# Splitting the feed-forward weights between the last projections instead of after them, in a fused attention and gated-cell kernel on one core

## The chip, the cores and the metric

One Trainium2 chip, of which the kernel uses one core. The time is device time in microseconds; a comparison is of medians of several runs. The profile is of one execution, taken by the hardware profiler.

## The reference, cut to what matters

Two layers run one after the other over 4096 tokens of width 256. The first is a linear attention with 16 heads of state size 64 whose causal weights are scaled by a decay and by a learned factor for the "level" of each pair (t, s). The second is a gated cell that runs two steps over the two halves of the tokens and then gives an output for each.

```python
Q, K, V, dl = x @ Wq.T, x @ Wk.T, x @ Wv.T, x @ Wdl.T      # per head
W = (Q K^T) * S**-0.5 * decay(t, s) * Lam[level(t, s)]      # causal
x = layernorm(x + layernorm(W V @ Wout.T + x) * g + b)
for xt in (x[0], x[1]):                                    # two steps
    f, i, g = sigmoid(xt@wf.T + c@uf.T + bf), sigmoid(xt@wi.T + c@ui.T + bi), tanh(xt@wc.T + c@uc.T + bc)
    c = f * c + i * g
x = layernorm(x + tanh(x @ wo.T + c @ uo.T + bo))
```

## The kernel before, in words

**Tiles and steps.** The tokens are cut into 32 chunks of 128 (`ci`, NC = 32) and 16 pairs of chunks (`sg`, NSG = 16). All engines run through the same list of steps `s` (STEPS, line 42), four per chunk, NG = 128 steps for the attention, and each engine's program is the order in which it does its part of a step. An engine works strictly in its own order: whatever a waiting instruction stands in front of waits too. PE is TensorE, ACT ScalarE, DVE VectorE, POOL GpSimd, SP the engine that issues every DMA.

**Attention, chunk ci, at step 4ci.** PE `exponents(ci)` (matmuls at L407) needs the transposed level coefficients CT of that chunk, made by DVE's `turn_levels(ci)`, and both halves of the weights W of the chunk before (`d_w`). ACT's `exps(ci)` turns them into E, PE does `weigh(ci-1)` (L439) and `keys(ci)` (transposes, L386), and at step 4ci+1 `scores(ci)` (QT, KT) once ACT has made the first two quarters of E. DVE multiplies scores and E in two halves, `weights(ci, 0)` at step 4ci+1 and `weights(ci, 1)` at 4ci+2. `inter(ci)` (PE L474, then DVE) adds what comes from earlier chunks, with coefficients cB that SP's `load_coefs(sg)` broadcasts from DRAM: one DMA of cT to a scratch (`scr`) and 16 DMAs of cB, issued one after the other, once ACT has written cT at step 8sg-3. `out_proj` (step 4ci+6) and `state(ci)` (PE L503, step 4ci+3) follow.

**Levels of a pair.** GpSimd's `levels(sg, 0)` and `levels(sg, 1)` make AT and prod for the even and the odd chunk of a pair; `token_jobs` puts them at distances 8 and 12 from step 8sg-11, so for the last pair (sg = 15) at steps 117 and 121. DVE's `turn_levels` comes a step later, at 118 and 122, each behind that step's `weights(ci, 1)`.

**Projections.** Q and K of pair sg are made in eight jobs (`project(sg, j)`), each with a product of split weights wH, wL (a high part and a remainder, so that three fast passes stand for one exact product). The last pair's are at steps 111 to 118. `split_x` splits the tokens of a pair out of the buffers xt[0] and xt[1].

**Feed-forward weights.** wH and wL hold the projection weights in the attention and the eight feed-forward matrices (WF, WI, WC, UF, UI, UC, WO, UO, numbers 0 to 7) after it, each in 256 columns. SP loads one matrix at a time into xt[0] or xt[1] (`load_wf`), ACT copies the high part into wH (`split_ffn`), GpSimd subtracts it into wL (`g_wf` counts these). Both do this at steps 119 to 126, matrix n at step 119 + n, at the end of the step. SP loads matrices 0 and 1 in its loop over the pairs, behind `load_coefs(13)` and `load_coefs(14)`, and 2 to 7 after the loop, behind `load_coefs(15)`.

**The seam.** At step 126 PE does `first_bias` (36 products two columns wide, which want six matrices split), at step 127 the first turns of the feed-forward blocks, and from step 128 its gates.

Of the kernel before, what the change touches and what calls it, by code (L numbers as in the profile page):

```python
# [5 lines left out]
P = 128  # L6
F32 = mybir.dt.float32
F32R = mybir.dt.float32r
ALU = mybir.AluOpType
ACT = mybir.ActivationFunctionType  # L10
# [5 lines left out]
NC = NT // P  # L16
# [25 lines left out]
STEPS = range(-3, NG + 13)  # L42
FIRST_FFN = NG - 1


def token_jobs(s):

    out = []
    for d, j in ((12, 7), (0, 0), (0, 1), (1, 2), (3, 8), (5, 3), (7, 4), (8, 5)):
        n = s + 11 - d  # L50
        if n % 8 == 0 and (0 if j == 7 else 1) <= n // 8 < NSG:
            out.append((n // 8, j))
    return out
# [12 lines left out]
def chunk_at(s, d):  # L66

    return (s - d) // 4 if s >= d and (s - d) % 4 == 0 and (s - d) // 4 < NC else None
# [87 lines left out]
def program(nc, x, xT, wqk, wtok, wout, wffn, cst, bcv, fv, out):  # L156
    ctx = ExitStack()
    with ctx:
# [139 lines left out]
        def wcol(n, mt=None):  # L298
            return slice(256 * n + 128 * mt, 256 * n + 128 * mt + 128) if mt is not None else slice(256 * n, 256 * n + 256)
# [4 lines left out]
        @block.sync  # L304
        def _(e):
            def load_x(sg):
                e.dma_start(xs[:, 2 * sg:2 * sg + 2, :], xv[:, 2 * sg:2 * sg + 2, :]).then_inc(l_x[sg], 16)

            def load_xt(sg):
                e.dma_start(xt[sg % 2][:, :, :], kt(xT)[:, :, 256 * sg:256 * sg + 256]).then_inc(l_xt[sg % 2], 16)  # L310

            def load_wf(n):
                e.dma_start(xt[n % 2][:, :, :], wffn.rearrange("(k p) w n -> p k w n", p=P)[:, :, n, :]).then_inc(
                    l_xt[n % 2], 16)

            def load_coefs(sg):

                m, u = MISC["cft", sg, 0]
                e.wait_ge(m_free[m], u + 1)
                e.dma_start(scr.rearrange("a l c t -> (a l) (c t)"), cT[:, :]).then_inc(l_sc, 16)  # L320
                e.wait_ge(l_sc, 16 * sg + 16)
                for c in range(2):
                    ci = 2 * sg + c
                    if ci in INTER:
                        if ci >= 2 and ci - 2 in INTER:
                            for h in range(2):
                                m, u = MISC["inter", ci - 2, h]
                                e.wait_ge(m_free[m], u + 1)
                        for a in range(8):
                            e.dma_start(cB[c][16 * a:16 * a + 16, :, :, :].rearrange("p l u t -> p (l u) t"),  # L330
                                        scr[a, :, c, :].partition_broadcast(16)).then_inc(l_cB[c], 16)

            load_xt(0)
            e.dma_start(wt0, kt(wtok)).then_inc(l_wt, 16)
            e.dma_start(bv[:, 0:B_G], bcv[:, 0:B_G]).then_inc(l_bv, 16)
            for i in (0, 2, 1, 3):
                for k in range(2):
                    c = slice(512 * i, 512 * i + 512)
                    e.dma_start(w0[k][:, c], kt(wqk)[:, k, c]).then_inc(l_wq[i], 16)
                if i == 2:  # L340
                    e.dma_start(cs[:, :], cst[:, 0:C_CT]).then_inc(l_cst, 16)
                    load_xt(1)
            e.dma_start(C[:, :, :].rearrange("p h l -> p (h l)"), cst[:, C_CT:C_END]).then_inc(l_c, 16)
            e.dma_start(wo[:, :, :], kt(wout)).then_inc(l_wo, 16)
            load_x(0)
            e.dma_start(bv[:, B_G:B_END], bcv[:, B_G:B_END]).then_inc(l_b2, 16)
            e.dma_start(fvs[:, :], fv).then_inc(l_b2, 16)
            load_x(1)

            e.wait_ge(p_proj, 8)  # L350
            load_xt(2)
            for sg in range(NSG):
                load_coefs(sg)
                if sg + 3 < NSG:
                    e.wait_ge(g_xl, sg + 1)
                    load_xt(sg + 3)
                if sg + 2 < NSG:
                    load_x(sg + 2)
                if sg >= NSG - 3 and sg < NSG - 1:
                    e.wait_ge(g_xl, sg + 1)  # L360
                    load_wf(sg - NSG + 3)
            for n in range(2, 8):
                e.wait_ge(g_wf, n - 1)
                load_wf(n)
            for n in range(16):
                e.wait_ge(a_out, n + 1)
                if n == 15:
                    e.wait_ge(d_out, 1)
                e.dma_start(ov[:, :, n, :], xs[:, n:n + 17:16, :]).then_inc(l_out, 16)
            e.wait_ge(l_out, 16 * 16)  # L370
# [5 lines left out]
        def wf_landed(n):  # L376
            return 16 * (NSG // 2 + n // 2 + 1)
# [3 lines left out]
        def _(e):  # L381
# [209 lines left out]
            def first_bias():  # L591

                e.wait_ge(a_qk, 8 * NSG)
                e.wait_ge(g_wf, UC + 1)
                e.wait_ge(g_c0, 1)
                for mt in range(2):
                    for n in range(3):
                        c, o = wcol(UF + n, mt), 2 * (3 * mt + n)
                        for k in range(2):
                            t = mm3(banks[0][:, o:o + 2], wH[:, k, c], wL[:, k, c], c0H[:, k, :], c0L[:, k, :],  # L600
                                    k == 0, k == 1)
                t.then_inc(p_b0, 1)
# [146 lines left out]
        def _(e):  # L749
            def act(o, i, f, **kw):  # L750
                return e.activation(o, i, f, **kw)  # L751
# [93 lines left out]
                        e.wait_ge(p_st, STATE[ci - 1] + 1)  # L845
                    act(Kt[:, 512 * n:512 * n + 512], MB[m][:, :], ACT.Copy).then_inc(m_free[m], 1)

            def split_ffn(n):
                e.wait_ge(l_xt[n % 2], wf_landed(n))
                if n == 0:  # L850
                    e.wait_ge(p_proj, 8 * NSG)
                act(wH[:, :, wcol(n)], xt[n % 2][:, :, :], ACT.Copy).then_inc(a_wf, 1)

            def turn_block(blk, t):
                i = blk % 2
# [83 lines left out]
            for s in STEPS:  # L939
                if 0 <= s < NG and s % 4 == 0:  # L940
                    exps(s // 4)
                if (sg := split_x_at(s)) is not None:
                    split_x(sg)
                if s == NG - 4:
                    act(c0H[:, :, :], bc(c0, 2, 2), ACT.Copy).then_inc(a_c0, 1)
                if 0 <= s < NG and s % 4 == 0:
                    keys(s // 4)
                for sg, j in project_jobs(s):
                    project(sg, j)
                for sg, j in token_jobs(s):  # L950
                    if j == 5:
                        turn_coefs(sg)
                for sg, j in token_jobs(s):
                    tokens(sg, j)
                if 0 <= s - NG + 9 < 8:
                    split_ffn(s - NG + 9)
                for u in units_at(s):
                    if u[0] == "x" and u[2] == 0:
                        gate(*u[1:])
                    elif u[0] == "c":  # L960
                        gate(u[1], 1, *u[2:])
                    elif u[0] == "h":
                        gate_h(*u[1:])
                    elif u[0] == "t":
                        turn_block(*u[1:])
                    elif u[0] == "o":
                        if u[1] < 16:
                            outputs(u[1])
                        if 0 <= u[1] - 2 < 16:
                            out_norm(u[1] - 2)  # L970
# [3 lines left out]
        def _(e):  # L974
# [34 lines left out]
            def weights(ci, u):  # L1009
                e.wait_ge(p_sc, 2 * ci + u + 1)  # L1010
                e.wait_ge(a_e, 4 * ci + 4)
                if ci:
                    e.wait_ge(p_y, 2 * ci + u - 1)
                for k in range(2):
                    hs = slice(8 * k + 4 * u, 8 * k + 4 * u + 4)
                    tt(W[:, hs, :], XP[2 * u + k][:, :].rearrange("p (h t) -> p h t", h=4), E[:, hs, :],
                       ALU.mult).then_inc(d_w, 1)
# [286 lines left out]
            for s in STEPS:  # L1304
                if (ci := chunk_at(s, 5)) is not None:
                    turn_y(ci)
                if 0 <= s < NG and s % 4 in (1, 2):
                    weights(s // 4, s % 4 - 1)
                for sg, j in token_jobs(s - 1):
                    if j in (5, 7):  # L1310
                        turn_levels(2 * sg + (j - 5) // 2)
                if (ci := chunk_at(s, 6)) is not None:
                    out_proj(ci)
                if s == FIRST_FFN:
# [32 lines left out]
        def _(e):  # L1347
# [104 lines left out]
            for s in STEPS:  # L1452
# [37 lines left out]
                if (ci := chunk_at(s, 9)) is not None:  # L1490
                    e.wait_ge(d_mv2, ci + 1)
                    root(rs2[:, :], lr2[:, :], mv2[:, 1:2], g_rs2)
                if 0 <= s - NG + 9 < 8:
                    n = s - NG + 9
                    e.wait_ge(a_wf, n + 1)
                    tt(wL[:, :, wcol(n)], xt[n % 2][:, :, :], wH[:, :, wcol(n)], ALU.subtract).then_inc(g_wf, 1)


def constants():
# [70 lines left out]
```

## Time and profile before

| what | value |
| --- | --- |
| median of 3 runs | 691.07 us (690.83 to 691.55) |
| the profiled execution's own time | 691.23 us |
| its span | 689.4 us |
| mean granted clock of PE over the span | 0.981 of full speed |
| PE busy | 667.5 us (97%) |
| DVE, ACT, POOL busy | 473.2 (69%), 339.6 (49%), 348.2 us (51%) |

The profiled execution takes 1.8 us more than its span, for what lies around it. The granted clock is 1.00 at 2.4 GHz and 0.50 at 1.2 GHz. A busy share is an average over stages with different limits, so the stage around the change is read by itself.

### The profile page before, as it was taken

What the parts mean: (1) busy time and instruction counts of PE and PEld (TensorE: products, weight loads), DVE (VectorE), ACT (ScalarE), POOL (GpSimd) and SP (SyncE); (2) the same over time, 40 slices, a digit from 0 to 9 for tenths busy, and PEclk for the clock granted to TensorE, in tenths of its full rate; (3) what the DMA queues carried; (4) which work ended last, traced back from release to release, by engine and by line L of the source; (5) the groups of instructions that cost most, each with busy time, mean ns of one, the idle gap of its engine ahead of it and who ended that gap; (6) DMA issues with size and microseconds to landing.
All of it is one profiled execution on the core that took longest, in us unless ns stands there. A gap on an engine that the chain in (4) does not pass through costs nothing.

```text
span 689.4 us, 22147 instructions
## 1 busy us (share of the span) xinstructions
PE 667.5 (97%) x9194; PEld 604.7 (88%) x9194; DVE 473.2 (69%) x1072; ACT 339.6 (49%) x759; POOL 348.2 (51%) x471
## 2 busy tenths in 40 slices
PE   9799999999999999999999999999978999999994
PEld 7699999999999999899999999999967888888894
DVE  3854877769786868667696868688896435454546
ACT  5545454445545554444455455545433434555555
POOL 2705555646465565656364655655455125343434
PEclk9999999999999999999999999999987899999998
DMA  8112130303131221203031212213032000000002
GB/s 303 40 45 58 41 88 11 98 7 94 30 70 41 60 57 42 68 2 98 8 91 32 68 48 52 69 31 82 3 98 63 1 1 1 31 31 31 31 32 92
DMA packets 53588, 37.09 MB, mean 54 GB/s; under 512 B 5360, under 2 KB 52080, under 8 KB 53488
## 3 DMA queue, kind: packets, MB, share of 16 engines
q1 hardware_dynamic: 53488, 35.67, 19.0%
q8 instruction: 73, 1.20, 0.8%
q14 instruction: 27, 0.22, 0.1%
HBM read 30.41 MB, written 5.24 MB: 52 GB/s over the span
## 4 chain that ended last, share of the span: by engine, by line
PE 90%; DVE 3%; ACT 2%; SPq 1%; DMA 1%; POOL 1%; issue 1%; POOLq 0%; DVEq 0%; ACTq 0%
PE bank L383 66%; PE bank L386 6%; PE bank L407 5%; PE bank L474 5%; PE bank L439 5%; PE bank L503 4%; SPq L330 1%; DMA xt<-in_wffn 1%; DVE t L982 1%; ACT t L751 0%; DVE st L1279 0%; DVE hh L979 0%; DMA scr<-cT 0%; DVE t L979 0%; ACT QT L751 0%
## 5 line engine op out<-in xcount | busy, mean ns | idle before, releaser
L383 PE MATMUL bank<-xH,wH 128*128 128x256 f32 x480 | 144.6, 301 | 0.0
L383 PE MATMUL bank<-xL,wH 128*128 128x256 f32 x480 | 135.0, 281 | 0.0
L383 PE MATMUL bank<-xH,wL 128*128 128x256 f32 x480 | 134.3, 280 | 0.0
L979 DVE TENSOR_TENSOR W<-bank,E 128x512 f32<-128x512 f32 x128 | 82.2, 684 | 34.7 <-PE bank L383 34.7
L383 PEld LDWEIGHTS bank<-xH,wH 128*128 128x128 f32 x480 | 90.5, 189 | 6.3 <-issue 5.5
L383 PEld LDWEIGHTS bank<-xL,wH 128*128 128x128 f32 x480 | 90.7, 189 | 0.4
L383 PEld LDWEIGHTS bank<-xH,wL 128*128 128x128 f32 x480 | 90.5, 188 | 0.0
L751 ACT ACTIVATE E<-bank 128x512 f32<-128x512 f32 x128 | 66.1, 603 | 49.0 <-PE bank L407 49.0
L751 ACT ACTIVATE QT<-bank 128x512 f32<-128x512 f32 x64 | 38.2, 596 | 100.7 <-PE bank L383 100.7
L383 PE MATMUL bank<-QT,KT 64*128 64x128 f32 x1024 | 65.9, 278 | 1.2 <-ACT E L751 1.2
L383 PEld LDWEIGHTS bank<-QT,KT 64*128 64x128 f32 x1024 | 59.7, 188 | 5.6 <-ACT E L751 1.5
L751 ACT ACTIVATE KT<-bank 128x512 f32<-128x512 f32 x64 | 38.0, 594 | 51.7 <-PE bank L383 51.7
L1351 POOL TENSOR_TENSOR lr<-mv,cs 128x1 f32<-128x1 f32 (+1 forms) x80 | 18.3, 228 | 80.8 <-DVE mv L1132 74.9
L1351 POOL TENSOR_TENSOR rs<-lr,cs 128x1 f32<-128x1 f32 (+1 forms) x80 | 51.7, 647 | 6.3
L1351 POOL TENSOR_TENSOR x<-oo,xs 128x256 f32<-128x256 f32 x32 | 23.5, 735 | 60.2 <-DVE oo L982 57.6
L1351 POOL TENSOR_TENSOR t<-t 128x416 f32<-128x416 f32 x42 | 46.6, 1110 | 3.4
L407 PE MATMUL bank<-CT,AT 32*128 32x128 f32 x1024 | 39.1, 291 | 9.3 <-ACT QT L751 5.2
L979 DVE TENSOR_TENSOR g<-g 128x512 f32<-128x512 f32 (+1 forms) x26 | 17.6, 677 | 38.7 <-ACT g L751 38.4
L407 PEld LDWEIGHTS bank<-CT,AT 32*128 32x128 f32 x1024 | 32.9, 193 | 10.6 <-DVE CT L1206 5.3
L1351 POOL TENSOR_TENSOR xL<-xt,xH 128x512 fp32r<-128x512 f32 x15 | 19.1, 1273 | 44.5 <-ACT xH L751 44.5
L751 ACT ACTIVATE t<-t 128x416 f32<-128x416 f32 x64 | 35.3, 552 | 12.6 <-DVE t L1164 7.8
L1351 POOL TENSOR_TENSOR prod<-ll,cs 128x512 f32<-128x512 f32 x32 | 40.7, 1271 | 1.2 <-DVE ll L979 1.2
(151 smaller groups left out, 1686.9 us busy)
## 6 DMA issues: line engine op xcount, KB each, us to landing
cB<-scr SPq DMA_DIRECT2D x240, 64.0 KB, 2.9
xt<-in_xT SPq DMA_DIRECT2D x16, 256.0 KB, 3.0
xs<-in_x SPq DMA_DIRECT2D x16, 256.0 KB, 3.2
out<-xs SPq DMA_DIRECT2D x16, 256.0 KB, 2.1
xt<-in_wffn SPq DMA_DIRECT2D x8, 256.0 KB, 3.1
QT<-in_wqk SPq DMA_DIRECT2D x4, 256.0 KB, 5.8
KT<-in_wqk SPq DMA_DIRECT2D x4, 256.0 KB, 6.1
scr<-cT SPq DMA_DIRECT2D x16, 64.0 KB, 1.9
```

Of the source, the lines that this page charges most:

```text
L330: e.dma_start(cB[c][16 * a:16 * a + 16, :, :, :].rearrange("p l u t -> p (l u) t"), scr[a, :, c, :].partition_broadcast(16)).then_inc(l_cB ...
L383: return e.matmul(o, a, b, start=start, stop=stop)
L386: return e.transpose(o, i, ident)
L407: m = e.matmul(XP[q][:, :].rearrange("p (h t) -> p h t", h=H)[:, :, 8 * j:8 * j + 8], AT[b][r, j, :], CT[b][r, :].rearrange("p (h t) -> p ...
L439: y = e.matmul(YB[32 * n:32 * n + 32, 128 * k:128 * k + 128], V[sg % 3][:, c, v:v + 32], W[:, h, :], start=u == 0 and k == 0, stop=u == 1, ...
L474: t = e.matmul(MB[MISC["inter", ci, k][0]][32 * n:32 * n + 32, 128 * i:128 * i + 128], S[r, l, n, 16 * o:16 * o + 32], QT[b][r, 4 * o + n, ...
L503: t = e.matmul(MB[m][k:k + 64, 16 * q:16 * q + 16], Kt[:, 128 * q + k:128 * q + k + 64], Vw[b][:, c, 128 * h + 16 * q:128 * h + 16 * q + 1 ...
L751: return e.activation(o, i, f, **kw)
L979: return e.tensor_tensor(o, a, b, op)
L982: return e.scalar_tensor_tensor(out=o, in0=a, scalar=s, in1=b, op0=op0, op1=op1)
L1351: return e.tensor_tensor(o, a, b, op)
```

## The change

The eight matrices are split at steps 112 to 119 rather than 119 to 126, in the order [0, 4, 1, 5, 2, 6, 3, 7], so that each goes to the columns which projection job i of the last pair has just read. SP issues loads 2 to 6 of this order ahead of `load_coefs(15)`, and load 7 behind it. For the last pair GpSimd makes the odd chunk's levels at step 119 (distance 10), DVE does both halves of `weights` at step 4ci+1 for the last two chunks, and the last `turn_levels` right behind them at step 121.

```diff
+FIRST_SPLIT = NG - 16
+SPLIT = [0, 4, 1, 5, 2, 6, 3, 7]
 def token_jobs(s):
     for d, j in ((12, 7), (0, 0), (0, 1), (1, 2), (3, 8), (5, 3), (7, 4), (8, 5)):
+        if j == 7 and s > NG - 12:
+            d = 10
         n = s + 11 - d
 # SP
-            def load_wf(n):
-                e.dma_start(xt[n % 2][:, :, :], wffn...[:, :, n, :]).then_inc(l_xt[n % 2], 16)
+            def load_wf(i):
+                if i >= 2:
+                    e.wait_ge(g_wf, i - 1)
+                e.dma_start(xt[i % 2][:, :, :], wffn...[:, :, SPLIT[i], :]).then_inc(l_xt[i % 2], 16)
             for sg in range(NSG):
+                if sg == NSG - 1:
+                    for i in range(2, 7):
+                        load_wf(i)
                 load_coefs(sg)
                 ...
-            for n in range(2, 8):
-                e.wait_ge(g_wf, n - 1)
-                load_wf(n)
+            load_wf(7)
 # PE, first_bias
-                e.wait_ge(g_wf, UC + 1)
+                e.wait_ge(g_wf, 7)
 # ACT
-            def split_ffn(n):
-                e.wait_ge(l_xt[n % 2], wf_landed(n))
-                if n == 0:
-                    e.wait_ge(p_proj, 8 * NSG)
-                act(wH[:, :, wcol(n)], xt[n % 2][:, :, :], ACT.Copy).then_inc(a_wf, 1)
+            def split_ffn(i):
+                e.wait_ge(l_xt[i % 2], wf_landed(i))
+                e.wait_ge(p_proj, 8 * (NSG - 1) + i + 1)
+                act(wH[:, :, wcol(SPLIT[i])], xt[i % 2][:, :, :], ACT.Copy).then_inc(a_wf, 1)
-                if 0 <= s - NG + 9 < 8:
-                    split_ffn(s - NG + 9)
+                if 0 <= s - FIRST_SPLIT < 8:
+                    split_ffn(s - FIRST_SPLIT)
 # DVE
-                if 0 <= s < NG and s % 4 in (1, 2):
+                if 0 <= s < NG - 8 and s % 4 in (1, 2):
                     weights(s // 4, s % 4 - 1)
+                if NG - 8 <= s < NG and s % 4 == 1:
+                    weights(s // 4, 0)
+                    weights(s // 4, 1)
                 for sg, j in token_jobs(s - 1):
-                    if j in (5, 7):
+                    if j == 5 or j == 7 and sg < NSG - 1:
                         turn_levels(2 * sg + (j - 5) // 2)
+                if s == NG - 7:
+                    turn_levels(NC - 1)
 # POOL
-                if 0 <= s - NG + 9 < 8:
-                    n = s - NG + 9
-                    e.wait_ge(a_wf, n + 1)
-                    tt(wL[:, :, wcol(n)], xt[n % 2][:, :, :], wH[:, :, wcol(n)], ALU.subtract).then_inc(g_wf, 1)
+                if 0 <= s - FIRST_SPLIT < 8:
+                    i = s - FIRST_SPLIT
+                    c = wcol(SPLIT[i])
+                    e.wait_ge(a_wf, i + 1)
+                    tt(wL[:, :, c], xt[i % 2][:, :, :], wH[:, :, c], ALU.subtract).then_inc(g_wf, 1)
```

## Rows read from the trace of the kernel before

**Rows 1.** Windows: length, busy us of PE, PEld, DVE, ACT, POOL; PE's clock; DMA.
```profile
440.00:505.00 65.00, 64.70 (x1201) 59.71 (x1200) 52.39 (x127) 30.80 (x71) 36.21 (x51) 1.00 0.20 51
505.00:540.00 35.00, 29.32 (x498) 25.32 (x498) 23.48 (x46) 12.96 (x24) 17.15 (x21) 0.76 0.25 70
540.00:680.00 140.00, 139.89 (x805) 121.52 (x803) 71.20 (x156) 69.35 (x131) 53.26 (x74) 1.00 0.06 21
...
530.00:540.00 10.00, 9.35 (x62) 7.72 (x62) 4.56 (x10) 3.67 (x5) 3.21 (x5) 0.50 0.01 2
```
**Rows 2.** Timeline of PE, steps 120 to 125: start, us, what, [idle before <-releaser].
```profile
502.82 1.17 PE L407 MATMUL bank<-CT,AT 32*128 32x128 f32 x32 [0.30 <-DVE CT L1206]
...
505.96 2.06 PE L383 MATMUL bank<-QT,KT 64*128 64x128 f32 x32
...
510.53 1.11 PE L503 MATMUL bank<-Vw,Kt 128*64 128x16 f32 x32
515.44 2.09 PE L407 MATMUL bank<-CT,AT 32*128 32x128 f32 x32 [3.80 <-DVE CT L1206]
517.46 1.94 PE L439 MATMUL bank<-W,V 128*32 128x128 f32 x32
519.33 1.29 PE L386 MATMUL bank<-cs,KT 128*128 128x128 f32 x8
521.85 2.13 PE L383 MATMUL bank<-QT,KT 64*128 64x128 f32 x32 [1.23 <-ACT E L751]
```
**Rows 3.** Timeline of DVE, steps 115 to 122.
```profile
490.36 0.41 DVE L1136 TENSOR_SCALAR xs<-x,mv,rs 128x256 f32<-128x256 f32 x1
...
504.77 1.44 DVE L1136 TENSOR_SCALAR xs<-x,mv,rs 128x256 f32<-128x256 f32 x1
...
507.38 1.28 DVE L979 TENSOR_TENSOR W<-bank,E 128x512 f32<-128x512 f32 x2
...
512.66 1.29 DVE L979 TENSOR_TENSOR W<-bank,E 128x512 f32<-128x512 f32 x2
...
514.67 0.71 DVE L1206 STREAM_TRANSPOSE CT<-C 128x512 f32<-128x512 f32 x1
```
**Rows 4.** Timeline of ACT, steps 117 to 124.
```profile
499.51 0.36 ACT L751 ACTIVATE cT<-bank 64x256 f32<-64x256 f32 x1
...
514.35 0.63 ACT L751 ACTIVATE wH<-xt 128x512 fp32r<-128x512 f32 x1 [6.74 <-DMA xt<-in_wffn]
...
520.19 0.63 ACT L751 ACTIVATE wH<-xt 128x512 fp32r<-128x512 f32 x1 [4.04 <-DMA xt<-in_wffn]
520.73 2.04 ACT L751 ACTIVATE E<-bank 128x512 f32<-128x512 f32 x4
```
**Rows 5.** Chain of work in order of time: step 116 at full clock, a weight load.
```profile
489.31 1.10 PE bank L407 x32
490.41 1.01 PE bank L439 x32
491.42 1.02 PE bank L386 x8
...
511.40 2.92 DMA xt<-in_wffn
```
**Rows 6.** Timeline of SP's queue: coefficients of the last two pairs, later loads.
```profile
470.14 8.79 SPq L330 DMA_DIRECT2D cB<-scr  x16
...
501.86 9.50 SPq L330 DMA_DIRECT2D cB<-scr  x16
511.40 14.70 SPq L313 DMA_DIRECT2D xt<-in_wffn  x6
```
**Rows 7.** Tile xt from 440 to 540: GpSimd's splits, the loads' landing (min/median/max).
```profile
L1351 POOL TENSOR_TENSOR wL<-xt,wH x8: 1267/1273/1535, 504.8 to 531.2; 128x512 fp32r<-128x512 f32 x8
...
DMA to landing us min/median/max: 2.8/3.1/4.7
```
**Rows 8.** Line L330, every coefficient DMA: ns to issue (min/median/max).
```profile
L330 SPq DMA_DIRECT2D cB<-scr x240: 303/431/1950, 30.6 to 510.9; - x120
```

More of the change, by code:

```diff
@@ L310, in load_xt @@
                 e.dma_start(xt[sg % 2][:, :, :], kt(xT)[:, :, 256 * sg:256 * sg + 256]).then_inc(l_xt[sg % 2], 16)
-            def load_wf(n):
-                e.dma_start(xt[n % 2][:, :, :], wffn.rearrange("(k p) w n -> p k w n", p=P)[:, :, n, :]).then_inc(
-                    l_xt[n % 2], 16)
+            def load_wf(i):
+                if i >= 2:
+                    e.wait_ge(g_wf, i - 1)
+                e.dma_start(xt[i % 2][:, :, :], wffn.rearrange("(k p) w n -> p k w n", p=P)[:, :, SPLIT[i], :]).then_inc(
+                    l_xt[i % 2], 16)
             def load_coefs(sg):
```

## The prediction

> **What bounds the kernel now.** I read windows first, then PE's timeline where it is not full, then who released it, then the queues behind those.
>
> The windows cut the span into attention, seam and feed-forward [rows 1]. PE is busy 64.70 of 65 us before 505 and 139.89 of 140 us after 540, at a granted clock of 1.00; only in the 35 us between them does it stand (29.32 busy) and run slow (0.76). No other engine is full anywhere: DVE has 52.39 of 65 us before 505. So work of ACT and GpSimd costs nothing while it is in time, and what a change can win or lose is in that seam.
>
> PE's timeline of the seam [rows 2] has two holes. The first: the last chunk's exponents stand 3.80 us, until 515.44, for CT. CT is made by the last `turn_levels`, whose transpose starts at 514.67, behind the second W half at 512.66, though the first half was made from 507.38 [rows 3]. The second: `scores(31)` wait 1.23 us, until 521.85, for ACT's E. ACT could have begun E at the end of the exponents but stood in its split of a weight matrix until the load landed: 6.74 us before 514.35, 4.04 us before 520.19, and only then E at 520.73 [rows 4]. The holes cost a third thing: the exponents, `weigh` and `keys` after the first hole take from 515.44 to 520.62 (521.85 less 1.23), 5.18 us, where the same three take 1.10 + 1.01 + 1.02 = 3.13 us at full clock [rows 2, 5]. That is 2.05 us at half the clock (1.2 of 2.4 GHz), right after PE had stood idle.
>
> Together 3.80 + 1.23 + 2.05 = 7.08 us. From `scores(30)` at 505.96 to `scores(31)` at 521.85 are 15.89 us; without the three it is 8.81.
>
> **Part 1: both W halves in step 121, the levels earlier.** The transposed CT of chunk 31 then needs W(30,0), W(30,1), the copy, reduce and transpose, and no longer stands behind `inter(30)` and the second step. From 507.38 that is 2 x 1.28 plus the 1.43 us from the second half's end (512.66 + 1.29) to the transpose's (514.67 + 0.71): ready at about 511.4, when PE's state products end (510.53 + 1.11 = 511.64) [rows 2, 3]. This takes out 3.80 us and the slow clock behind it, 2.05. The d_w wait of the exponents is met at the same moment. Late next is nothing on DVE: DVE's `inter(30)` moves behind 1.3 + 1.4 us of other work, and so does its `state(30)`, which PE's `inter(31)` waits for; but PE has exponents, `weigh`, `keys` and `scores` (3.13 + 2.1 us) in between. Cost zero, with that work as cover, and up to 2.7 us if it is gone.
>
> **Part 2: eight splits moved to steps 112 to 119.** Each issues one ACT copy (0.63 us), one GpSimd subtraction (1.27 us) and one load on SP [rows 4, 7]. ACT gets 5 us and GpSimd 10.2 us more within about 30; they were busy 30.80 and 36.21 of 65 [rows 1]. The gates of loads 2 to 6 are a turn-around of split, load and split, 1.27 + 3.1 + 0.63 = 5.0 us per two steps, and a step is some 3 us (four of them from 502.82 to 515.44 with the hole), so it just keeps up; I let ACT wait up to 1 us in it, which PE's projections hide. With those splits gone from steps 120 to 126, the 1.23 us before `scores(31)` go too.
>
> **Part 3: load 7, and what queues behind it.** This is what decides. SP does its loads in program order: 2 to 6, then `load_coefs(15)`, then 7. `load_coefs(15)` starts when ACT has written cT at 499.51 and ends with 16 issues, 9.50 us from 501.86 to 511.36; the next in the queue, a weight load, is issued at 511.40 [rows 4, 6]. That place, held by matrix 2 before, is now load 7's. It lands 2.92 us later, at 514.33 [rows 5]. But ACT wants it at step 119 and stands there, and behind it in ACT's order are `exps(30)` of step 120, which followed the exponents of 502.82 at once before. Everything of chunk 30 hangs on them:
> - ACT's split at 514.35, next instruction 0.54 later (520.19 to 520.73), so E(30) at 514.89;
> - scores 1.12 after E starts (520.73 to 521.85), so `scores(30)` at 516.01 [rows 2, 4], against 505.96: **+10.05 us**, in which PE has nothing to do (its exponents, `weigh` and `keys` are done by 506);
> - then 8.81 us of work, plus slow clock after a 10 us hole. The hole of 3.80 cost 2.05; I take the same, so `scores(31)` at 526.87 against 521.85: **+5.02 us**.
>
> So the sum is 10.05 - 3.80 - 1.23 - 2.05 + 2.05 = +5.02. From `scores(31)` on both kernels have the same PE work to the first gate; `first_bias` now asks for seven splits, which were done long before. The feed-forward part is full of PE work and only moves. GpSimd's split 7 waits with ACT and holds x1 of chunk 28, whose reader on DVE stands behind W(30) anyway.
>
> **Unknown terms, from both sides.** The 16 issues took 8.79 us for the pair before [rows 6]: -0.7 us. Should ACT's inserted copies make cT late: +0.6 to +1. Landing 2.8 to 4.7 us [rows 7]: -0.1 to +1.8; I take 2.92, the same place in the queue. The slow clock could last longer after a longer hole: at worst as in 530 to 540, where all 10 us ran at 0.50 [rows 1], which is 5 us rather than 2.05, +3; the short stretch is nearer, since dense work follows in both. That slow stretch itself, behind the two-column products of `first_bias`, I keep at its 5 us; were PE back at full clock 4 us after the turns begin, as after the first hole, about 2.5 us come back, and all of it at best.
>
> **Two DVE durations against a rule.** A DVE operation took 0.41 us alone and 1.44 us while GpSimd split a matrix [rows 3]: +1.03. The Trainium skill ("SBUF — State Buffer", section "SBUF: two separate sides") calls the port pair that DVE and GpSimd share an exclusive lock: a GpSimd operation that starts first fully blocks a DVE one with two SBUF inputs. The row agrees in kind; the rule would let each of the eight splits hold DVE for its whole length, 10.2 us, and it speaks against moving them to where PE is full.
>
> **The rivals.**
> - A. *DVE is late before step 117.* Six splits fall there, and at 1.03 us each that is 6.2 us on DVE [rows 3]. DVE's idle share, 12.6 of 65 us, gives back 5.0 of some 26 us [rows 1]. Between 1.2 and 6.2 us would reach PE and shift cT, the coefficients and all that follows; I take 2 us, near the lower end, since PE's dependences on DVE there have steps of slack. Time 691.1 + 5.0 + 2.0 = 698.1. Against: splits after step 117 hide in the new hole.
> - B. *The clock comes back at the seam.* PE is busy longer before `first_bias`, and the slow stretch is shorter or absent: 691.1 + 5.0 - 2.5 = 693.6, or 691.1 with all 5 us back. For: its start is not fixed by a wait. Against: its cause, tiny products, stays.
> - C. *Faster: load 7 is in time.* If it is landed when these exponents end, all of 7.08 us is won: 684.0. The point from which it decides: gain and loss balance when `scores(30)` start 7.08 - 2.05 = 5.03 us late, at 510.99, so with a landing at 509.3. Even with all 16 issues at their fastest, 0.303 + 0.04 us each [rows 8], 5.5 us, load 7 goes out at 507.4 and lands at 510.2. So this needs the queue to be shorter than the code has it, or to combine with B.
> - D. *It does not do what it says*: ACT's wait is covered by something I missed, and the time stays at 691.1.
>
> **How the numbers follow.** The profiled execution (span 689.4, own time 691.23) would become 694.4 and 696.3; it stands 0.16 above the median of 691.07, so the forecast is 691.07 + 5.0 = **696.1 us**. Chances: forecast 0.64, A 0.14, B 0.12 (half of it within 0.2%), C 0.07, D 0.03. A measurement of this kernel tells changes of over 0.2%, 1.4 us. Faster 0.07; same 0.06 + 0.03 = 0.09; slower 0.64 + 0.14 + 0.06 = 0.84. The range takes the forecast with its bounds (-0.8 for the queue, +1.8 for the landing or as much for the clock), A, and the nearer half of B: 693.0 to 699.3; the far half of B, C and D are left out.
>
> **What would show it.** In the profile after: ACT's eighth split starts at about 514.3 with an idle time of 10 to 12 us before it, released by the DMA; PE stands about 10 us before `scores(30)`, put down to ACT's E; no hole before the last L407 group and none before `scores(31)`; a granted clock of 0.50 for some 4 us after 516; the first gate at about 543 instead of 537.9; the feed-forward part as long as before. A hole before 499 would speak for A; an eighth split before 510, or a SP queue that issues it ahead of the cB group, would make the forecast wrong, as would a granted clock of 1.00 right after the hole.

## The result, and the profile after

The changed kernel takes 696.73 us (median of 4 runs, 695.15 to 698.45) against 691.01 us before, a ratio of 1.0082 (95% interval 1.0055 to 1.0109). It is slower by 5.7 us; forecast were 5.0 and 696.1 us. Built and timed a second time it took 697.59 against 691.34 us, 1.0092 (1.0077 to 1.0107).

Of the profiled execution (698.45 us, span 696.7) 2.26 us have nothing to do with the change: the exponents of chunk 29 already start that much later, at 491.50 instead of 489.24 (in the chain of waits 489.31 [rows 5]). Some of it is there at the first exponents of all, where no line differs (35.68 against 34.74 us), behind a load of constants that was awaited until 7.79 us instead of 6.87; and the clock after them was half for longer (mean 0.90 from 40 to 50 us, against 1.00). So I compare **the seam**: from the start of the exponents of chunk 29 to the first gate product. It is 48.70 us before (489.24 to 537.94) and 53.93 after, +5.23.

The windows of after, the seam's end moved with the rest (columns as in [rows 1]):

```profile
440.00:505.00 65.00, 64.79 (x1152) 60.05 (x1150) 53.65 (x124) 34.46 (x79) 42.79 (x55) 1.00 0.25 69
...
505.00:545.00 40.00, 31.49 (x552) 27.92 (x556) 25.56 (x54) 9.78 (x19) 11.53 (x18) 0.73 0.14 35
545.00:685.00 140.00, 140.00 (x804) 121.25 (x797) 69.42 (x151) 68.33 (x128) 51.23 (x70) 0.99 0.06 20
```

Before 505 ACT and GpSimd have 3.7 and 6.6 us more work and PE is as full as it was; after 545 nothing has changed. The loss is in the seam, where PE now stands for 8.5 of 40 us instead of 5.7 of 35. The timeline of PE in it, to be read against [rows 2]:

```profile
491.50 1.17 PE L416 MATMUL bank<-CT,AT 32*128 32x128 f32 x32
...
506.16 2.09 PE L416 MATMUL bank<-CT,AT 32*128 32x128 f32 x32 [1.37 <-DVE CT L1214]
508.18 1.74 PE L448 MATMUL bank<-W,V 128*32 128x128 f32 x32
509.85 1.09 PE L395 MATMUL bank<-cs,KT 128*128 128x128 f32 x8
517.56 3.78 PE L392 MATMUL bank<-QT,KT 64*128 64x128 f32 x32 [6.62 <-ACT E L760]
521.27 2.46 PE L483 MATMUL bank<-QT,S 64*32 64x128 f32 x96
...
524.73 1.11 PE L512 MATMUL bank<-Vw,Kt 128*64 128x16 f32 x32
525.77 1.17 PE L416 MATMUL bank<-CT,AT 32*128 32x128 f32 x32
...
529.19 2.05 PE L392 MATMUL bank<-QT,KT 64*128 64x128 f32 x32
...
545.43 0.80 PE L392 MATMUL bank<-yH,wH 128*128 128x512 f32 x1
```

Both old holes are gone (no wait stands before 525.77 and 529.19). A small one before the exponents of chunk 30 has grown from 0.30 to 1.37 us. A new one of 6.62 us stands before `scores(30)`, released by ACT's E, and the work after it runs slowly: 3.78 us for products that take 2.06. What ACT and SP did meanwhile, from their timelines:

```profile
504.28 0.62 ACT L760 ACTIVATE wH<-xt 128x512 fp32r<-128x512 f32 x1
515.91 0.63 ACT L760 ACTIVATE wH<-xt 128x512 fp32r<-128x512 f32 x1 [11.01 <-DMA xt<-in_wffn]
516.44 2.04 ACT L760 ACTIVATE E<-bank 128x512 f32<-128x512 f32 x4
```
```profile
502.17 0.46 SPq L328 DMA_DIRECT2D scr<-cT  x1
504.13 8.76 SPq L338 DMA_DIRECT2D cB<-scr  x16
512.93 0.43 SPq L321 DMA_DIRECT2D xt<-in_wffn  x1
```

ACT waits 11.01 us for the eighth matrix, whose load SP issues at 512.93, behind the 16 coefficient DMAs. E follows 0.53 us after the split starts, and the scores 1.12 us after E.

### The profile page after: what moved, and what is told of

Read it like the earlier page. It is cut to its first block, busy times and chain, and to the rows that moved or that the text cites. A ratio compares the mean times of both kernels' runs of the same rounds, so it can differ in the third digit from the quotient of the medians.

```text
span 696.7 us, 22154 instructions
## 1 busy us (share of the span) xinstructions
PE 671.2 (96%) x9194; PEld 608.6 (87%) x9194; DVE 474.9 (68%) x1072; ACT 338.9 (49%) x759; POOL 348.5 (50%) x471
## 4 chain that ended last, share of the span: by engine, by line
PE 90%; DVE 3%; ACT 2%; DMA 2%; SPq 1%; issue 1%; POOL 1%; POOLq 0%; DVEq 0%; ACTq 0%
PE bank L392 65%; PE bank L395 6%; PE bank L416 5%; PE bank L483 5%; PE bank L448 5%; PE bank L512 4%; SPq L338 1%; DMA bv<-in_bcv 1%; DVE t L990 1%; ACT t L760 0%; DMA xt<-in_wffn 0%; DVE st L1287 0%; DVE hh L987 0%; DMA scr<-cT 0%; DVE t L987 0%
## 5 line engine op out<-in xcount | busy, mean ns | idle before, releaser
L392 PE MATMUL bank<-QT,KT 64*128 64x128 f32 x1024 | 67.5, 283 | 6.6 <-ACT E L760 6.6
L392 PEld LDWEIGHTS bank<-QT,KT 64*128 64x128 f32 x1024 | 61.3, 192 | 11.0 <-ACT E L760 7.0
L392 PE MATMUL bank<-yH,wH 128*128 128x512 f32 (+1 forms) x102 | 40.2, 394 | 0.0
```

Source lines behind the costliest of these rows:

```text
L392: return e.matmul(o, a, b, start=start, stop=stop)
```

## The experiments

The theory: ACT's order puts E of chunk 30 behind a split that waits for a load which is last in SP's queue. Its rivals: DVE and GpSimd, loaded by the moved splits, are the bound; or the part that should win is worth something else than its hole. The table gives each run's seam beside its time, and how much of the seam lies ahead of `scores(31)`; the start of a run scatters by a microsecond or two, the seam of two profiles of the same kernel by 0.36. Before and the kernel in question ran on the same chip each time.

| kernel | time, before beside it | ratio (95%) | seam, us | up to `scores(31)` |
| --- | --- | --- | --- | --- |
| before | | | 48.70 | 32.61 |
| changed | 696.73, 691.01 | 1.0082 (1.0055 to 1.0109) | 53.93 | 37.69 |
| changed, again | 697.59, 691.34 | 1.0092 (1.0077 to 1.0107) | 54.29 | 37.61 |
| load 7 between | 693.51, 690.63 | 1.0032 (1.0014 to 1.0049) | 50.75 | 34.05 |
| split 7 late | 689.48, 690.63 | 0.9983 (0.9968 to 0.9998) | 46.32 | 31.58 |
| levels only | 691.83, 690.63 | 1.0013 (0.9999 to 1.0027) | 48.38 | 32.79 |
| splits only | 699.36, 690.63 | 1.0124 (1.0097 to 1.0151) | 56.92 | 42.18 |
| split 7 late, old levels | 689.36, 691.34 | 0.9970 (0.9959 to 0.9980) | 46.37 | 31.62 |
| split 7 late, inter first | 688.28, 691.34 | 0.9968 (0.9946 to 0.9990) | 47.90 | 30.88 |
| split 7 late, no subtraction | 687.12, 691.34 | 0.9954 (0.9931 to 0.9977) | 46.38 | 31.64 |
| DVE relieved | 687.10, 690.23 | 0.9956 (0.9943 to 0.9970) | 42.56 | 27.81 |

Behind `scores(31)` every kernel gives PE the same work, and yet this part took 14.74 us in some profiles and up to 17.02 in others. The first line is from the kernel before, the second from the run with split 7 late:

```profile
530.09 0.35 PE L383 MATMUL bank<-c0H,wL 128*128 128x2 f32 x1
530.59 0.25 PE L397 MATMUL bank<-c0H,wL 128*128 128x2 f32 x1
```

In the kernel before, the two-column products start at 526.71 and PE is at half clock from about 530.0, before they end; in the other they start at 526.58 and all 36 are done at full clock. Behind `scores(31)` the two differ by 1.35 us (16.09 and 14.74), and 1.21 of it lie between the first of these products and the gate. So the part up to `scores(31)` is the better measure of what an edit did, and each seam is that of one execution only.

**1. The eighth split out of ACT's way.**

```diff
+def split_at(s):
+    i = s - FIRST_SPLIT
+    return [i] if 0 <= i < 7 else [7] if s == NG - 2 else []
-                if 0 <= s - FIRST_SPLIT < 8:        # ACT and GpSimd
+                for i in split_at(s):
```

> The changed kernel with one edit: ACT and GpSimd do the split of the eighth matrix at step 126 instead of 119, so nothing of ACT stands behind the last load when chunk 30 needs its E. Theory (ACT's order behind load 7 is what costs): the 6.6 us hole before scores(30) is gone, scores(30) follow keys(30) at once; the hole of 1.4 us before the exponents of chunk 30 and the half clock behind it stay, so of the 7.08 us that the change takes out some 4.4 are won: 686.6 us (685.0 to 688.5). Rival A (DVE or GpSimd, loaded with the moved splits, hold chunk 30): a hole of over 4 us stays before scores(30) or inter(30), and the time stays above 693.

The seam falls from 53.93 to 46.32 us, the part up to `scores(31)` from 37.69 to 31.58, and the kernel is now 1.2 us faster than before: 0.17%, less than the 0.2% taken as told apart, though the interval just leaves out 1. `scores(30)` follow `keys(30)` without a wait, so the order on ACT was the cause. But the time is 2.9 us above what I expected, and PE's timeline says why:

```profile
504.48 1.17 PE L421 MATMUL bank<-CT,AT 32*128 32x128 f32 x32 [0.92 <-DVE CT L1219]
...
507.68 2.06 PE L397 MATMUL bank<-QT,KT 64*128 64x128 f32 x32
...
514.90 1.89 PE L517 MATMUL bank<-Vw,Kt 128*64 128x16 f32 x32 [2.58 <-DVE zt L992]
516.72 2.09 PE L421 MATMUL bank<-CT,AT 32*128 32x128 f32 x32
518.75 1.94 PE L453 MATMUL bank<-W,V 128*32 128x128 f32 x32
```

A new hole of 2.58 us stands before `state(30)`: its bank is free only when DVE has read the products of `inter(30)` out of it (zt). Ahead of that read now stand both halves of W, 2.5 us, and 1.4 us of levels, where one half stood before. After it the clock is half again. In the changed kernel no such hole is seen, but `state(30)` starts as late there, 7.17 us after `scores(30)` against 7.22 here and 4.57 in the kernel before: PE spends the same time on `scores` and `inter` at half clock.

**2. A dose: the same load behind 8 DMAs instead of 16.**

```diff
                 for c in range(2):                  # SP, load_coefs
+                    if sg == NSG - 1 and c:
+                        load_wf(7)
-            load_wf(7)                              # SP, behind the loop
```

> The changed kernel with load 7 issued between the two halves of the last pair's coefficient DMAs, that is behind 8 of them instead of 16. Theory: a dose. Load 7 goes out some 4.2 us earlier, lands as much earlier, scores(30) start as much earlier, and the time falls by the same: 692.5 us (691.5 to 693.5). Rival (the hole is set by something other than the landing): no change, 696 to 697; rival (landing is not set by its place in SP's queue but by transfers in flight): load 7 goes out earlier but lands at the same time.

```profile
503.07 4.79 SPq L340 DMA_DIRECT2D cB<-scr  x8
507.92 0.42 SPq L321 DMA_DIRECT2D xt<-in_wffn  x1
508.45 3.88 SPq L340 DMA_DIRECT2D cB<-scr  x8
```

Counted from the exponents of chunk 29, the load goes out 17.47 us on instead of 21.43 and `scores(30)` start at 22.43 instead of 26.06: 3.96 us earlier at one end, 3.63 at the other; ACT's split behind it starts 3.63 us earlier too (20.78 us on instead of 24.41). The part up to `scores(31)` falls by 3.64, the whole seam by 3.2 (3.5 against the second profile), the time by 3 to 4 us. Place in SP's queue sets the landing, and the landing the hole.

**3. Each part alone.** The first is the kernel before with step 121's new order on DVE and the odd levels at 119; the second the changed kernel without them.

```diff
+        if j == 7 and s > NG - 12:                  # levels only: added to before
+            d = 10
 ...
+                if NG - 8 <= s < NG and s % 4 == 1:
+                    weights(s // 4, 0)
+                    weights(s // 4, 1)
+                if s == NG - 7:
+                    turn_levels(NC - 1)
```

> The kernel before with the other part alone: odd levels of the last pair at step 119, both W halves and the last turn of levels in step 121; the eight splits stay at steps 119 to 126. Theory: the exponents of chunk 31 start at about 511.7 with no hole, but ACT still stands in its splits for loads until 520.2, so scores(31) still start at about 521.9 behind a hole of about 7 us: the time is as before, 691.0 us (690.2 to 692.3). Rival (the 3.8 us hole was worth its length): 685 to 688.

> The changed kernel with the other part undone: odd levels at step 121, W halves in steps 121 and 122, the last turn at 122; the splits stay between the projections. Theory: the 6.6 us hole before scores(30) is there as in the changed kernel, and behind it CT of chunk 31 is late again, by what DVE does between (inter(30), its sum, the statistics): 2 to 4 us of hole before the exponents of chunk 31. Time 699.5 us (698 to 702). Rival (the earlier levels were needed by nothing once chunk 30 is late): 696 to 697.3, as the changed kernel.

Levels only: the seam is 0.32 us shorter, all of it behind `scores(31)`, and the time is not told from that of before. PE's timeline has both holes still, the first under another name:

```profile
514.59 1.90 PE L506 MATMUL bank<-Vw,Kt 128*64 128x16 f32 x32 [2.90 <-DVE zt L982]
...
523.11 2.13 PE L386 MATMUL bank<-QT,KT 64*128 64x128 f32 x32 [1.30 <-ACT E L754]
```

I had expected the hole to sit before `scores(31)`, 7 us long; it is 2.90 us before `state(30)` and 1.30 behind. The time came out as expected, the mechanism only half. Splits only: 699.36 us, seam 56.92, 2.6 to 3.0 us worse than the changed kernel and 4.5 us worse up to `scores(31)`, with 3.23 us of hole before the exponents of chunk 31. So the levels part does earn something in the changed kernel, where its price, the late `state(30)`, lies under the half clock.

**4. The levels part with ACT free.** As experiment 1, with the second part undone.

> As the run with the late split, but with the other part of the change undone (odd levels at step 121, W halves in steps 121 and 122, last turn of levels at 122). It measures what that part is worth when ACT no longer stands. Theory: little, since it only moves a hole on DVE from before the exponents of chunk 31 to before state(30): a hole of 3 to 4.5 us before the exponents, the seam 46 to 47.5 us, the time within 1 us of the late split's. Rival (the part is worth the 3.8 us hole it was made for): seam 49 to 51 us.

Seam 46.37 against 46.32, and 31.62 against 31.58 up to `scores(31)`: the part is worth nothing here. Its 3.23 us of hole before the exponents of chunk 31 (the wait of L418 in this run) are the other form of experiment 1's 2.58 before `state(30)`.

**5. Two misses.** Both add to experiment 1. The first moves DVE's read of `inter(30)` between the two W halves; the second shrinks GpSimd's subtractions.

```diff
                     weights(s // 4, 0)              # inter first
+                    if s // 4 == NC - 2:
+                        inter_products(s // 4)
                     weights(s // 4, 1)
 ...
-  tt(wL[:, :, c], xt[i % 2][:, :, :], wH[:, :, c], ALU.subtract)                           # no subtraction
+  tt(wL[:, :, c][:, :, 0:1], xt[i % 2][:, :, 0:1], wH[:, :, c][:, :, 0:1], ALU.subtract)
```

> The changed kernel with the eighth split at step 126 (as in the run with the late split) and one more edit: DVE does the products of inter(30) between the two W halves of chunk 30, not behind W and the turn of levels. Theory (with the hole before E gone, the next thing late is the state product of chunk 30, which waits for DVE to read inter(30) out of its bank): the 2.6 us hole before state(30) shrinks to under 1 us, the exponents of chunk 31 start some 1.2 us earlier and at full clock; the seam is 42.5 to 45 us and the time 2 to 3.5 us under the late split's. Rival (DVE's work as a whole is the bound there, whatever its order): the hole moves on to the exponents of chunk 31, the seam stays at 45.5 to 46.5 us.

> As the run with the late split, but GpSimd's eight subtractions work on one column of 256 each (the remainders of the feed-forward weights are left out, all waits and counts stay). It measures what GpSimd's moved work costs. Theory (shared port and late levels delay DVE by some 3 us between steps 116 and 121): DVE's operations that took 1.25 to 1.5 us beside GpSimd fall to 0.4 to 0.8, the 0.9 us hole before the exponents of chunk 30 goes, the one before state(30) shrinks; the seam falls from 46.3 to about 43 us. Rival (GpSimd's work is hidden): 46 us, as with the subtractions.

Inter first: the hole moved on, as its rival had it. The one before `state(30)` is gone, and instead:

```profile
516.53 2.09 PE L421 MATMUL bank<-CT,AT 32*128 32x128 f32 x32 [1.99 <-DVE CT L1224]
```

The half clock came with it. Up to `scores(31)` this is still 0.70 us better than experiment 1; the seam of 47.90 is 1.6 us longer because the part behind took 17.02 us against 14.74, with the clock at half before the two-column products end. The timed ratio does not separate it from experiment 1. No subtraction: the seam did not move (46.38), and DVE's two long operations were as long as before; the hole before `state(30)` is 2.00 us instead of 2.58, the one before the exponents of chunk 30 1.29 instead of 0.92.

For these two kernels a single profile says too little. Of ten executions without the subtractions six took 685.60 to 687.26 us, at a mean clock of 0.985 to 0.987, and four 690.34 to 690.90 us at 0.981; the profiled one is of the four. With inter first it was six of 685.96 to 688.71 us (0.983 to 0.987) and four of 691.13 to 691.71 us (0.978), the profiled one again among the four. Of ten with split 7 late two took less than 688.5 us. Outside the seam the eleven profiled spans have 640.1 to 642.8 us; if the six without subtractions had at least 640.1 there, their seams were at most 43.7 to 45.4 us (an estimate from their spans of 683.8 to 685.5 us). So what the subtractions cost is not shown: nothing in the profile, but the median is 2.4 us under that of experiment 1, and the intervals of the two ratios overlap by little.

What DVE's two operations stood beside was something else, seen when the timelines of DVE and GpSimd in the changed kernel are laid side by side:

```profile
508.23 1.25 DVE L1144 TENSOR_SCALAR xs<-x,mv,rs 128x256 f32<-128x256 f32 x1
509.40 1.47 DVE L990 SCALAR_TENSOR_TENSOR oo<-oo,mv,bv 128x256 f32<-128x256 f32 x1
510.91 0.48 DVE L990 SCALAR_TENSOR_TENSOR oo<-oo,rs,bv 128x256 f32<-128x256 f32 x1
```
```profile
508.24 1.09 POOL L1365 TENSOR_TENSOR AT<-cs,cgt 128x512 f32<-128x512 f32 x1
509.29 1.30 POOL L1365 TENSOR_TENSOR prod<-ll,cs 128x512 f32<-128x512 f32 x1
```

Each long operation ends just after one of the two GpSimd operations of `levels(15, 1)`, which the change itself had brought forward from step 121 to 119. This is the lock of which the Trainium skill speaks ("SBUF — State Buffer", section "SBUF: two separate sides"): the one that starts first holds the shared port pair for its whole instruction, and the other is blocked. The rows fit the second pair, where GpSimd was first by 0.11 us; in the first pair the recorded starts are 0.01 us apart and do not tell who was first.

The same happens once more, earlier. Behind its subtractions, which wait for ACT's splits, GpSimd ends `levels(15, 0)` 12.5 us after the exponents of chunk 29 instead of 9.2. The first line is from the kernel before, the others from the changed one:

```profile
499.13 0.42 DVE L979 TENSOR_TENSOR zs<-zt 128x256 f32<-128x256 f32 x1
```
```profile
501.69 1.20 DVE L987 TENSOR_TENSOR zs<-zt 128x256 f32<-128x256 f32 x1
501.33 1.28 POOL L1365 TENSOR_TENSOR AT<-cs,cgt 128x512 f32<-128x512 f32 x1
```

Here GpSimd was first by 0.36 us. With 0.29 us on the operation before it (0.71 instead of 0.42), that is the 1.08 us by which the exponents of chunk 30 come later (14.66 us after those of chunk 29, against 13.58). In the second profile of the changed kernel and in experiments 1 and 4, DVE waits 0.44 or 0.45 us for the second operation of these levels (prod) instead, and the exponents come 0.62 to 0.64 us later. Levels only, without the moved splits, has 13.59.

**6. A version that beats both.** The split late, the odd levels back at 121 (beside W, which reads PSUM), and `inter(30)` read behind both W halves but ahead of the last turn of levels.

```diff
-        if j == 7 and s > NG - 12:
-            d = 10
 ...
                     weights(s // 4, 1)
+                    if s // 4 == NC - 2:
+                        inter_products(s // 4)
```

> The changed kernel with the eighth split at step 126, GpSimd's odd levels of the last pair back at step 121 (so they no longer run beside two-input operations of DVE at step 119 and 120, which took 1.25 and 1.47 us there instead of 0.41 and 0.48), and DVE's products of inter(30) behind both W halves but ahead of the last turn of levels. Theory (before the last exponents DVE's queue is the bound, and what it loses beside GpSimd is 1.8 us of it): W of chunk 30 starts some 1.5 us earlier against scores(30), the holes before state(30) and the exponents of chunk 31 are under 1 us each, PE stays at full clock through exponents, weigh and keys: seam 42 to 44.5 us instead of 46.3, the time 3 to 5 us under the kernel before. Rival (a hole of over 1 us stays somewhere and the half clock with it, as it moved on in the three runs before): seam 45.5 to 47 us.

```profile
505.70 0.41 DVE L1151 TENSOR_SCALAR xs<-x,mv,rs 128x256 f32<-128x256 f32 x1
506.03 0.48 DVE L992 SCALAR_TENSOR_TENSOR oo<-oo,mv,bv 128x256 f32<-128x256 f32 x1
...
507.98 2.48 DVE L989 TENSOR_TENSOR W<-bank,E 128x512 f32<-128x512 f32 x4 [0.62 <-PE bank L394]
```
```profile
503.63 1.17 PE L418 MATMUL bank<-CT,AT 32*128 32x128 f32 x32 [1.36 <-DVE CT L1221]
...
506.77 2.06 PE L394 MATMUL bank<-QT,KT 64*128 64x128 f32 x32
...
512.92 1.18 PE L418 MATMUL bank<-CT,AT 32*128 32x128 f32 x32 [0.47 <-DVE CT L1221]
514.65 1.08 PE L450 MATMUL bank<-W,V 128*32 128x128 f32 x32 [0.55 <-DVE oo L989]
```

DVE's two operations are back at 0.41 and 0.48 us, and W, now beside the levels, is not held (2.48 us for its four, 2.47 in experiment 1). W follows the scores at once, the holes are 0.47 and 0.55 us and the exponents run at full clock. The seam is 42.56 us, 6.1 less than before, 4.80 of it up to `scores(31)`; the time is 687.10 against 690.23 us, 0.9956 (0.9943 to 0.9970). The median gains 3.1 us and the profiled execution (684.48 us) was the fastest of six, so the seam of this one may be better than most. Its executions spread over 3.6 us, and the clock goes with them: 0.988 in the profiled one, 0.986 in two, 0.983 in the slowest three (687.46 to 688.09 us). What sets that stays open, what each of its edits brings was not run separately, and its ratio is not told from those of experiments 4 and 5.

## Why the prediction was right, point by point

- **What bounds.** That the seam alone decides is right: the feed-forward part is 140.00 of 140 us busy, 139.89 before.
- **Part 3, +10.05 us at `scores(30)`.** Right in mechanism, shown by experiments 1 and 2. Measured from the exponents of chunk 29 it is 26.06 less 16.72, +9.34 us; the term was too large by the 16 issues, 8.76 us instead of 9.50, which was the lower bound given. ACT's idle time was 11.01 us (10 to 12 said). PE's own wait is 6.62 us rather than 10, since its work before came later and at half clock: 1.37 us of wait for CT of chunk 30 stand before it. In the second profile, without the slow stretch, it is 8.49.
- **The slow clock, 2.05 us.** Too small: `scores` and `inter` of chunk 30 took 3.71 and 2.39 us from start to start where they took 1.98 and 1.53, so 2.59. With 0.2 us of small delays the way to `scores(31)` is 11.63 us, not 10.86. The two errors, -0.7 and +0.8, cancel; that the sum of 5.02 meets the seam's 5.23 so closely is partly luck.
- **Part 1, "Late next is nothing on DVE. Cost zero".** This step was wrong, though it did not show in the result. I took `inter(31)` as the next reader of DVE and overlooked that `state(30)` waits for its bank: it starts 7.17 us after `scores(30)` instead of 4.57, and the half clock on `scores` and `inter`, 2.59 us, happens to cover the same time. That is luck too. Its price is in experiments 1 and 3: 2.58 to 2.90 us of hole and half clock after it, nearly all of what the part takes away. The gain of 7.08 us that I set against the loss, and rival C's 684.0 us, were not to be had by freeing ACT alone: that gave 689.5 us, with 1.03 us less up to `scores(31)`.
- **Part 2.** ACT waited 1.80 us before its fourth split (up to 1 said), hidden as said. What GpSimd's subtractions cost is not shown (experiment 5).
- **Rivals.** A fell as to its size, not its kind: before 505 PE is 64.79 of 65 us busy, but CT of chunk 30 is late by 0.6 to 1.1 us in the profiles with the moved splits (experiment 5), which the wait for load 7 hides. The 10.2 us that I had set beside the sum for the eight splits did not come: DVE is 53.65 of 65 us busy before 505, against 52.39. Nor does the row of 1.44 us say who was first: DVE's start is recorded at 504.77, GpSimd's at 504.79. B fell for this kernel: the slow stretch behind the two-column products came as before (from about 537 to 547), and `scores(31)` to the first gate took 16.24 us against 16.09. In five of the other profiles that part took 14.74 or 14.75 us, so a shorter loss there, as B has it, does occur, by 1.35 us. C and D fell with the result. The rest of the measured 5.7 to 6.3 us over the seam's 5.2 to 5.6 is the start's scatter, of which the runs say no more.

## What to carry to other kernels

When a step is moved earlier on an engine, ask for every wait in it where its releaser stands in its own queue: here seven of eight loads stood ahead of the last 17 coefficient DMAs and one did not, and an engine that waits in order passed that one load's lateness on to everything behind it. When a stall is removed by reordering an engine, list all who wait for what was pushed back, buffer releases too; a hole that comes back under another name can mean that the engine's total work is the bound, and then less of it (here, not beside the other user of the port) is worth a try. Compare executions by a stretch around the change when the start scatters as much as the effect, and look where the profiled execution lies among the timed ones before its stretch is taken for the kernel's.

## What the runs showed of the hardware that I had not expected

A hole's length did not decide whether the clock fell. A wait of 1.37 us in the changed kernel was followed by exponents of 2.09 us (half clock); one of 1.36 us in the last version, and those of 0.92 us and 1.02 us in others, by 1.17 us. A slow stretch was not tied to its hole in length either: after 3.80 us of wait PE ran slow for some 4 us, after 6.62 us for nearly 6, and after 1.99 and 2.58 us (experiments 5 and 1) for some 6. So the clock is part of the scatter: executions of one unchanged kernel had mean clocks of 0.981 to 0.987 and lay up to 5.3 us apart (without the subtractions, 685.60 to 690.90 us).
